# Second cross attention: row sums from the exponentials, weights normalised by GpSimd instead of the output by VectorE

## The reference

```python
def proj(x, w):
    return (x @ w.T).reshape(B, -1, H, D_K).transpose(0, 2, 1, 3)
query = proj(q, w_q)
key_ = proj(k, w_k)
value = proj(v, w_v)
scores = jnp.einsum('bhqd,bhkd->bhqk', query, key_) / jnp.sqrt(jnp.asarray(D_K, dtype=query.dtype))
scores = jnp.where(mask == 0, jnp.asarray(NEG, dtype=scores.dtype), scores)
attn = jax.nn.softmax(scores, axis=-1)
out = jnp.einsum('bhqk,bhkd->bhqd', attn, value)
out = out.transpose(0, 2, 1, 3).reshape(B, -1, H * D_K)
return out @ w_o.T
```

## Time and profile before

| | us |
|---|---|
| median of 3 runs | 1636.38 |
| lowest and highest run | 1633.44, 1636.63 |
| span of the profiled execution | 1668.7 |
| PE busy | 1493.5 (90% of the span) |
| DVE busy | 1233.5 (74%) |
| ACT busy | 1124.9 (67%) |
| POOL busy | 912.9 (55%) |
| the second cross attention, first to last copy to `c_pT` | 631.5 to 905.1 |

### The profile page before, as it was taken

How to read it: one execution, slowest core, us unless ns; L and a number is a source line. 1 busy time by engine, 2 the same in 40 slices (tenths; PEclk the granted TensorE clock), 3 DMA queues, 4 the chain that set the end, 5 groups by cost and what they waited for, 6 DMA issues and landing times.

```text
span 1668.7 us, 38570 instructions
## 1 busy us (share of the span) xinstructions
PE 1493.5 (90%) x12380; PEld 1229.8 (74%) x12443; DVE 1233.5 (74%) x3032; ACT 1124.9 (67%) x2663; POOL 912.9 (55%) x789
## 2 busy tenths in 40 slices
PE   4899999899868989888896899999889899999888
PEld 3677777677757767666674788888767688888766
DVE  6888888788756557777774788888656777877656
ACT  4878888688744547677674678778633678778632
POOL 4667777777740114444431777777500777777500
PEclk8999999999998999999998899999999999999999
DMA  9700000000022330100000000000000000000000
GB/s 382 302 2 7 11 13 10 10 15 12 13 64 67 86 96 26 33 16 16 15 12 6 11 16 14 15 15 14 10 12 4 6 16 14 15 16 14 9 18 38
DMA packets 75553, 61.29 MB, mean 37 GB/s; under 512 B 40256, under 2 KB 61120, under 8 KB 74688
## 3 DMA queue, kind: packets, MB, share of 16 engines
q1 hardware_dynamic: 71360, 51.69, 9.6%
q0 software_dynamic: 4096, 8.40, 1.7%
HBM read 21.30 MB, written 30.41 MB: 31 GB/s over the span
## 4 chain that ended last, share of the span: by engine, by line
PE 58%; DVE 21%; ACT 10%; issue 6%; POOL 4%; DMA 1%; DVEq 0%; SPq 0%; POOLq 0%; ACTq 0%
PE slot L1634 6%; PE slot L458 5%; PE slot L460 4%; PE slot L459 4%; PE slot L1617 4%; PE slot L1578 4%; PE slot L1587 3%; PE slot L1313 3%; ACT a_p L733 3%; PE slot L1652 3%; DVE a_sum L850 3%; POOL a_rq L1096 3%; PE slot L1868 3%; PE slot L1364 2%; DVE a_ssq L958 2%
## 5 line engine op out<-in xcount | busy, mean ns | idle before, releaser
L1035 POOL TENSOR_TENSOR rs<-mv,nhalf 128x1 f32 (+1 forms) x160 | 99.5, 622 | 276.7 <-DVE mv L1030 209.5
L1784 POOL TENSOR_TENSOR d_A<-d_A,d_B 128x1024 f32<-128x1024 f32 x64 | 150.7, 2354 | 134.3 <-DVE d_B L1730 134.3
L1788 POOL TENSOR_TENSOR d_r<-d_vv,nhalf 128x16 f32<-128x16 f32 x64 | 186.5, 2914 | 47.9 <-DVE d_vv L1752 47.4
L733 ACT ACTIVATE d_p<-slot,d_nm,d_r 128x128 f32<-128x128 f32 x512 | 186.0, 469 | 25.9 <-DVE d_nm L1743 25.9
L733 ACT ACTIVATE a_p<-slot,a_nm,a_rq 128x77 f32<-128x77 f32 x512 | 163.9, 434 | 54.4 <-DVE a_nm L758 54.4
L1634 PE MATMUL slot<-d_v,d_pT 128*128 128x65 f32 x1024 | 121.8, 272 | 1.4 <-ACT d_pT L1671 1.4
L733 ACT ACTIVATE c_p<-slot,c_nm 128x77 f32<-128x77 f32 x512 | 117.5, 362 | 7.6 <-DVE c_nm L1419 4.7
L1634 PEld LDWEIGHTS slot<-d_v,d_pT 128*128 128x128 f32 x1024 | 119.4, 192 | 2.1 <-ACT d_pT L1671 1.8
L740 POOL TENSOR_TENSOR a_p<-a_p,a_rc 128x616 f32<-128x616 f32 x64 | 80.1, 1252 | 72.2 <-DVE a_rc L852 71.7
L1711 DVE TENSOR_TENSOR d_A<-slot,T 128x1024 f32<-128x1024 f32 x64 | 78.4, 1225 | 49.0 <-PE slot L1578 48.7
L1389 ACT ACTIVATE c_pT<-slot 77x1024 f32<-77x1024 f32 x64 | 65.7, 1027 | 69.1 <-PE slot L1313 68.9
(11 more groups left out here) (284 smaller groups left out, 4602.5 us busy)
## 6 DMA issues: line engine op xcount, KB each, us to landing
routed<-zero SPq DMA_DIRECT2D x2, 9216.0 KB, 49.3
b_x<-routed SPq DMA_DIRECT2D x80, 64.0 KB
answers<-b_y SPq DMA_DIRECT2D x40, 128.0 KB
X<-in_x SPq DMA_DIRECT2D x2, 1024.0 KB, 7.7
d_zx<-Z SPq DMA_DIRECT2D x64, 32.0 KB
H<-Z SPq DMA_DIRECT2D x64, 32.0 KB
out<-f_o SPq DMA_DIRECT2D x8, 256.0 KB, 2.0
d_zx<-Z SPq DMA_DIRECT2D x64, 31.8 KB
```

Of the source, the lines that this page charges most:

```text
L733: i = e.activation(t["p"][:, h, :], R[slot][:, k // nbank, nk * (k % nbank):nk * (k % nbank) + nk], ACT.Exp, bias=t["nm"][:, h:h + 1], sca ...
L1035: return e.tensor_tensor(rs[:, bass.ds(b, 1)], mv[:, bass.ds(b, 1), 1:2].rearrange("p a b -> p (a b)"), nhalf[:, 0:1], ALU.pow)
L1784: e.tensor_tensor(t["A"][:, p, :], t["A"][:, p, :], t["B"][:, p, :], ALU.add).then_inc(S("d_key"), 1)
L1788: e.tensor_tensor(t["r"][:, it.m(2, 4), :], t["vv"][:, p, :], nhalf[:, 0:16], ALU.pow).then_inc(S("d_key"), 1)
```

## The change

The tile `onesz` and the products with it go. Each exponential instruction of this part also gives the sum of what it wrote (`accum_out`), into spare columns of the PSUM bank whose scores it read. VectorE inverts eight such sums per half (`shares`, tile `c_rc`). GpSimd multiplies `c_p` in place with the reciprocals (`normed`, semaphore `c_pn`), and the transposes wait for that. VectorE only copies the output (`c_oT`) from PSUM. ScalarE's exponentials of half 0 move ahead of its second copy to `c_pT`.

```diff
@@ exponentials @@
-        def exponentials(e, t, slot, half, nbank, nk, done, scale=None, head=lambda h: h):
+        def exponentials(e, t, slot, half, nbank, nk, done, scale=None, head=lambda h: h, total=None):
...
-                                 bias=t["nm"][:, h:h + 1], scale=1.0 if scale is None else scale[:, head(h):head(h) + 1])
+                                 bias=t["nm"][:, h:h + 1], scale=1.0 if scale is None else scale[:, head(h):head(h) + 1],
+                                 accum_out=None if total is None else total[:, k:k + 1])
@@ c_tensor @@
+        totals = [R[2 + half][:, 1, 4 * SK:4 * SK + 8] for half in range(2)]
...
-                        e.wait_ge(S(("ac_expa", "ac_expb")[half]), count(b, base=NB))
+                        e.wait_ge(S("c_pn"), count(b, half + 1, 2))
...
-                        if half == 0:
-                            if it.seen(5):
-                                e.wait_ge(S("ac_expa"), it.upto(5, NB))
-                        else:
-                            if it.seen(5):
-                                e.wait_ge(S("ac_expb"), it.upto(5, NB))
+                        if it.seen(5):
+                            e.wait_ge(S("c_rc"), nth(it.upto(5), half + 1, 2))
...
-                    for j in range(4):
-                        for g in range(4):
-                            mm = e.matmul(R[0][32 * g:32 * g + 32, 1, 384:512],
-                                          onesz[0:SK, j, :, :].rearrange("p a b -> p (a b)"), t["pT"][0:SK, 4 * g + j, :],
-                                          start=(j == 0), stop=(j == 3))
@@ c_scalar @@
-                b = it.b(5)
-                if b is not None:
-                    for half in range(2):
-                        e.wait_ge(S(("ac_PTa", "ac_PTb")[half]), count(b, base=NB))
+                b4, b5 = it.b(4), it.b(5)
+                for half in range(2):
+                    if b5 is not None:
+                        e.wait_ge(S(("ac_PTa", "ac_PTb")[half]), count(b5, base=NB))
...
-                b = it.b(4)
-                if b is not None:
-                    p = {"p": t["p"][:, it.m(4, 2), :, :], "nm": t["nm"]}
-                    e.wait_ge(S("ac_mxa"), count(b, base=NB))
-                    exponentials(e, p, 2, 0, 4, SK, S("ac_expa"))
+                    if half == 0 and b4 is not None:
+                        p = {"p": t["p"][:, it.m(4, 2), :, :], "nm": t["nm"]}
+                        e.wait_ge(S("ac_mxa"), count(b4, base=NB))
+                        exponentials(e, p, 2, 0, 4, SK, S("ac_expa"), total=totals[0])
...
-                    exponentials(e, p, 3, 1, 4, SK, S("ac_expb"))
+                    exponentials(e, p, 3, 1, 4, SK, S("ac_expb"), total=totals[1])
@@ c_vector @@
+            def shares(b, half):
+                h = slice(8 * half, 8 * half + 8)
+                e.wait_ge(S(("ac_expa", "ac_expb")[half]), count(b, base=NB))
+                if past(b - 1):
+                    e.wait_ge(S("c_pn"), count(b - 1, half + 1, 2))
+                e.reciprocal(t["rc"][:, h], totals[half]).then_inc(S("c_rc"), 1)
...
+                b = it.b(5)
+                if b is not None:
+                    shares(b, 1)
...
+                b = it.b(4)
+                if b is not None:
+                    shares(b, 0)
...
-                    e.reciprocal(t["rcT"][:], R[0][:, 1, 384:512]).then_inc(S("c_rcT"), 1)
-                    e.wait_ge(S("c_rcT"), count(b3))
-                    e.tensor_tensor(t["oT"][:, it.m(5, 2), :], R[0][:, 1, 0:128], t["rcT"][:], ALU.mult).then_inc(S("ac_oTe"), 1)
+                    e.tensor_copy(t["oT"][:, it.m(5, 2), :], R[0][:, 1, 0:128]).then_inc(S("ac_oTe"), 1)
@@ c_pool @@
+            def normed(b, half, m):
+                h = slice(8 * half, 8 * half + 8)
+                p = c_["p"][:, m, h, :]
+                e.wait_ge(S("c_rc"), count(b, half + 1, 2))
+                apart(e)
+                e.tensor_tensor(p, p, c_["rc"][:, h].unsqueeze(2).to_broadcast([128, 8, SK]), ALU.mult)\
+                    .then_inc(S("c_pn"), 1)
...
+                b = it.b(5)
+                if b is not None:
+                    normed(b, 1, it.m(5, 2))
...
+                b = it.b(4)
+                if b is not None:
+                    normed(b, 0, it.m(4, 2))
```

More of the change, by code:

```diff
@@ L150, in program @@
         maskb = at("maskb", [128, 4, SK], BF16)
-        onesz = at("onesz", [128, 4, 4, DH1])
         nhalf = at("nhalf", [128, 32])
@@ L285, in program @@
         c_["p"] = at("c_p", [128, 2, 16, SK])
[L286 removed]
+        c_["rc"] = at("c_rc", [128, 16])
         c_["pT"] = at("c_pT", [128, 16, 128])
@@ L402, in split_dve @@
             e.wait_ge(S("eps"), 3)
-            e.memset(onesz[:], 0.0).then_inc(S("const"), 1)
             e.memset(a["kb"][:], 0.0).then_inc(S("const"), 1)
@@ L413, in split_dve @@
             e.tensor_tensor(a["wqk"][:], nrm0[:, 0:1], nrm0[:, 1:2], ALU.mult).then_inc(S("const"), 1)
-            e.wait_ge(S("const"), 4)
-            for j in range(4):
-                e.memset(onesz[:, j, j, :], 1.0).then_inc(S("c_const"), 1)
         def first_stats(e, n):
@@ L471, in a_tensor @@
             e.wait_ge(S("split"), 2)
-            e.wait_ge(S("const"), 4)
+            e.wait_ge(S("const"), 3)
             e.wait_ge(S("counted"), 9)
```

5 lines of the change are left out of this document (2 added, 3 removed).

## The result

The changed kernel takes **1750.84 us** (median of 4 runs, 1749.38 to 1756.53), the kernel before 1634.91 beside it: ratio **1.0723** (1.0695 to 1.0751), 116 us slower. The forecast was 1709 with 1664 to 1742 as its range, so the direction was right and the size was not: the time lies 9 us above the range.

What follows compares the result with a forecast made beforehand. TensorE was read as leading, VectorE close behind; the change would close a ring of 9.60 us per step. Loops 22, weight splits 2, other steps 10 and 3, fill and drain 3: 40 on 1668.7 gives 1709 us, range 1664 to 1742.

Steps and rivals of the forecast that it cites:

- The ring of 9.60: Looped step: VectorE's last statistic, root of i-6, multiply of half 1, its transposes and scores, back through VectorE; 9.60 us.
- The base: Time the added 40 us stands on: the profiled span of 1668.7, rather than the median run of 1636.4.
- the gaps: TensorE idle between products with `onesz`, 1.49 us per looped step; inferred to belong to the profiled execution, not to runs.
- rival of 1676: The 9.60 us steps as summed, but gaps in runs too, so 1636.4 + 40 = 1676; chance 0.24.
- The sums: ScalarE's 16 exponentials per step also write sums; extra time taken as 0.10 us each, adding nothing to the step.
- `e`: Extra time of one ScalarE exponential that also writes its sum: taken as 0.10 us, between 0 and 0.30.
- GpSimd's multiply and VectorE's reciprocal: Added work per half, priced from the first cross attention: multiply 1.22 us, reciprocal of eight sums 0.20 us.
- The clock: Rival: TensorE's clock falls from waits, half speed in every third step, 20 us more, 1729; chance 0.18 with dear sums.
- dear sums: Rival: each exponential's sum costs 0.30 us on ScalarE, step 10.8, 37 us more, 1746; chance 0.18 together with the clock.
- A clock under 0.95: Sign of being wrong: TensorE's granted clock in the changed stage under 0.95.
- The rest of the sum: Outside looped steps: 10 us for steps 5, 6, 7, 32; 3 for steps 33 to 35; about 3 for fill and drain.
- Handoffs that hide: Rival: last root and multiply of half 1 run while TensorE is at half 0; step 7.6, 1610; faster 0.07.

Runs made afterwards that it cites:

- e13: e5 without the 8 unread products ahead of the transposes of half 1; 1700.44 us, ratio 1.0398.
- e1: The changed kernel with the products with `onesz` kept on TensorE, unread; ratio 1.0383 for three runs (1730.87, 1739.44, 1750.06 us), 1768.95 us in the fourth.
- e14: e13 with GpSimd's root of block i-6 moved behind the next step's first multiply; 1696.19 us, ratio 1.0372.
- e8: The kernel before, unchanged, run and profiled again on a chip where it takes 1635; 1635.34 us, ratio 0.9993.
- e2: The kernel before, with the exponentials of the second cross attention also writing their sums, which nobody reads; 1678.72 us, ratio 1.0052.
- e5: The changed kernel with unread bf16 products (24, 8 and 16) on TensorE in front of its waits; 1701.45 us, ratio 1.0408.
- e11: The kernel of e3 again, on a chip where the kernel before takes 1635; 1635.38 us, ratio 1.0010.
- e7: The changed kernel, unchanged, run again on the same chip as e5; 1752.10 us, ratio 1.0712.
- e6: The changed kernel with the second cross attention's transposes and everything behind them one step later; 1685.52 us, ratio 1.0319.
- e9: e6 with unread products on TensorE, 8 ahead of each group of transposes and 24 ahead of the products with the values; 1669.62 us, ratio 1.0220.
- e12: e5 with GpSimd's root of block i-6 moved behind the next step's first multiply; 1701.45 us, ratio 1.0413.
- e3: The kernel before without the products with `onesz`, normalisation left out; 1648.72 us, ratio 0.9866.

## Why the prediction was wrong

**The ring of 9.60: right, with a twin.** At full clock the step is 9.28 to 9.93 (e13) or 9.56 to 9.94 (e1), on both sides of the forecast. Each term of the sum is found in the fence above. What the sum missed is a second ring of nearly the same length, through the mixing, the root of `i-1`, the context copy and the multiply of half 0. Its pieces, those of the turn in the first section, are 3.72 + 1.26 + 2.29 + 2.01 = 9.28 us in e14 at full clock, where TensorE waits 0.31 us for ScalarE's first copy between the groups. At full clock it hides behind the first (e13) or, where that is shortened, takes its place (e14).

**The base: right in size, wrong in cause.** The forecast said that runs do the looped steps without gaps, in about 7.2, and that the gaps are the profiler's. The kernel before does them in 7.45, with a span of 1634.1, on the one chip of the three at 1635 where it was profiled (e8); on the fourth chip it takes 1670, and the profile of e2 shows the gaps. The profile that the forecast was made from has the span of the fourth chip's executions; where it was taken isn't known. The Trainium skill's page "NOTIFIC — the notification-queue block", section "7.1 Overflow: three behaviours, one of which stalls the engine", says that a full queue of records can, in one of its settings, stall the engine that produces them, and was weighed for this. No run here shows such a stall, and the runs of e2 are not shorter than its span. What decides that a chip has the gaps stays open. With the base of the chips without gaps the count works: 24 x (9.60 - 7.2) = 58 us is what the forecast's steps give for the loops, 57.3 was measured (e5: 24 x (9.84 - 7.45)), and the change without its loss of clock is e13 and e5, 1700 and 1701, against the forecast 1709 and its rival of 1676. That 1709 comes so near is in part luck: base and terms were each off by some us. The forecast also read TensorE as the leading engine, close ahead of VectorE; with the gaps gone VectorE sets the undisturbed steps (e11).

**The sums: right.** Eight take 2.08 us instead of 1.67, each counted to the next instruction's start, so `e` is 0.05 (0.10 was taken, 0.30 the upper end), and e2 costs 0.5%. The Trainium skill's page "VectorE: DVE Perf Modes", section "Two Vector instructions with no wait between them", counts an operation that also writes out its accumulator as two instructions. The trace shows the same form on ScalarE: the read is a row of its own, 0.16 to 0.29 us long in these eight. But most of it lies beside the next exponential, so its length is not its price.

**GpSimd's multiply and VectorE's reciprocal: right**, 1.21 and 0.21 us where 1.22 and 0.20 were priced.

**The clock: the step that failed.** The sum of 1709 has nothing for it, as every term is taken at full clock. It was a rival, together with dear sums, at 0.18, and priced at 20 us: half speed in every third step, 2.02 us of the ring twice as long. A clock under 0.95 in the stage was also named as a sign of being wrong, and it was 0.61. It cost 51 us (1752.5 - 1701.1): 42.5 in the 24 steps, 7.4 before and 1.5 behind them. Two terms of that price were too small.

- *How often.* The clock was low for 70 to 78% of the looped stage, not for a third. The forecast saw the clock fall after one step with 3 us of gaps, and saw that the new steps have 3.4 us of waits each, yet took a third of them without a row for it. Once low it stayed low: steps 8 to 13 of the changed kernel stand at 0.50 throughout, although TensorE works about 11.2 us of each and waits 0.9 to 1.6.
- *What of TensorE stands in the ring.* At half clock the twin ring takes over, and it has all four groups of TensorE in it, not one half's: 3.50 + 3.61 us instead of 2.29 + 2.01, so a step of 12.09 instead of 9.28, 2.81 more and not 2.02.

By the forecast's own form, 0.70 x 24 x 2.6 (e7's share of half clock; 12.09 less a full-clock step of some 9.5) = 44 us for the 24 steps, against 42.5 measured. The share is a measured one; no row of before gave it.

**The rest of the sum**: without the clock the change costs 67 us of span on the chips without gaps, 57.3 in the looped steps, 6.9 ahead and 2.7 behind. The forecast's terms beside the looped steps, on the same side of that line, were 10 for steps 5, 6, 7 and 32 with 3 for the last three and 3 for fill and drain: 16, where 10 were measured.

**Handoffs that hide: no.** TensorE's wait for the multiply stood in every looped step; e6 shows what it took to hide it, a whole further step of lag, and even that left 50 us.

## What to carry to other kernels

Where TensorE is the busiest engine but another engine or a ring sets the step, work taken off TensorE buys nothing (e11: 0.1%), and waits put in its way can cost it the clock (51 us here). Sum every ring twice, once with TensorE's pieces at each of its two speeds: the ring that governs at half speed can be another one. Here the half-speed sum of 12.09 gives an upper estimate for the loops, 24 x (12.09 - 9.60) = 60 us over the forecast; how much of it comes true hangs on how often the clock is low, which only the runs showed (0.70 to 0.78 of the time). A filler of unread products is a probe for the clock (50 us here), but look what it stands in front of, for it can become the bound (e9) or hide the ring that one wants to see (e12).

## What was unexpected of the hardware

- The clock stays low under a busy TensorE. In the changed kernel TensorE worked 239.48 of 281.24 us, 85%, and was granted 0.61. In e6 it worked 14.00 of 14.00 us at 0.50. Ahead of these 14 us it had waited 2.15 us for ScalarE; in the changed kernel no wait of the looped steps for a multiply was longer than 2.8 us.
- The same program differs by chip, by 2% (1635 against 1670). Between the profile that the forecast was made from and e8 it is 34.6 us of span, of which 29.6 lie in the 24 looped steps, with gaps of 0.40 to 0.46 us among dense small products. TensorE's idle time put down to "issue" between 660 and 860 us was 17.7 us in e2, all of it among the `onesz` products; e3, without them, had 4.9 us on that chip, elsewhere, and e1, which has them but waits for GpSimd in each step, 3.6 us. The gaps are not all of the difference: the kernel without these products takes 1648.72 there (e3) and 1635.38 on another chip (e11). Where these 13 us lie stays open.
- A sum written by an exponential of 128x77 costs 0.05 us, though its row is 0.23 us long on average, since most of it lies beside the next exponential.
